# Expert phase of a gated cross-attention chain: 21 blocks of 128 places in place of 14 of 256, weights as the moving operand, the product back in whole fp32

## What is computed

```python
x = hidden_states.reshape(-1, HIDDEN)                 # 896 rows of 256, layer-normed
probs = softmax(30 * tanh(x @ wg.T / 30))             # 8 experts
topk_vals, topk_ids = top_k(probs, 2)
topk_w = topk_vals / sum(topk_vals)
h1 = einsum('th,eih->tei', x, w1)                     # w1, w3: 8 x 1024 x 256
h3 = einsum('th,eih->tei', x, w3)
act = gelu(h1) * h3
out = einsum('tei,ehi->teh', act, w2)                 # w2: 8 x 256 x 1024
# x += tanh(g) * sum of the two chosen experts' rows, weighted
```

## Time and profile before

| | us |
|---|---|
| median of 3 runs | 1394.43 (1383.29 to 1396.78) |
| the profiled execution | 1392.34 |
| span of its instructions | 1390.6 |
| PE busy | 1204.5 (87%) |
| DVE busy | 857.2 (62%) |
| ACT busy | 672.0 (48%) |
| POOL busy | 532.2 (38%) |

### The profile page before, as it was taken

The page is one execution under the profiler, slowest core; times in us unless marked ns, Lnnn a source line. Parts: engine busy times, 40 slices in busy tenths (PEclk is TensorE's granted clock), DMA queues, the critical chain, the costliest instruction groups (busy, mean ns, idle before and its releaser), DMA issues. The chain is left out here.

```text
span 1390.6 us, 25468 instructions
## 1 busy us (share of the span) xinstructions
PE 1204.5 (87%) x9571; PEld 954.4 (69%) x9571; DVE 857.2 (62%) x1973; ACT 672.0 (48%) x1512; POOL 532.2 (38%) x536
## 2 busy tenths in 40 slices
PE   3999999999997697689999469889888859999876
PEld 2677777777775265556777469889887747777544
DVE  6664555555554346667787556666666476777676
ACT  3355444455452221257666234554454136666565
POOL 3355554555553000288887431110100441271132
PEclk9999999999998798889999579999999979999987
DMA  6000000000001151300110355556662260000000
GB/s 181 12 2 12 12 1 12 12 1 1 2 1 29 30 157 41 91 22 23 44 32 2 126 189 167 189 173 200 182 198 83 61 192 24 13 13 2 1 7 21
DMA packets 60090, 88.96 MB, mean 64 GB/s; under 512 B 8673, under 2 KB 49905, under 8 KB 59969
## 3 DMA queue, kind: packets, MB, share of 16 engines
q1 hardware_dynamic: 57856, 81.82, 19.3%
q0 software_dynamic: 2112, 5.51, 1.4%
HBM read 81.81 MB, written 5.51 MB: 63 GB/s over the span
## 5 line engine op out<-in xcount | busy, mean ns | idle before, releaser
L906 POOL TENSOR_SCALAR a_arena<-a_arena 112x487 f32<-112x487 f32 x128 | 192.7, 1516 | 176.9 <-DVE a_arena L1117 176.9
L1198 ACT ACTIVATE a_arena<-banks,a_arena 112x487 f32<-112x487 f32 x128 | 84.2, 663 | 193.0 <-DVE a_arena L1111 193.0
L1111 DVE TENSOR_REDUCE a_arena<-banks 112x2 f32<-112x974 f32 x64 | 75.0, 1172 | 102.6 <-PE banks L997 102.6
L93 PE MATMUL banks<-f_x_high,f_up_high 128*128 128x256 f32 x448 | 128.4, 287 | 3.6 <-DVE f_up_low L2010 2.2
L94 PE MATMUL banks<-f_x_low,f_up_high 128*128 128x256 f32 x448 | 128.0, 286 | 0.0
L95 PE MATMUL banks<-f_x_high,f_up_low 128*128 128x256 f32 x448 | 128.0, 286 | 0.0
L397 POOL TENSOR_TENSOR a_arena<-a_arena 112x375 f32<-112x375 f32 x128 | 114.7, 921 | 24.1 <-ACT a_arena L704 23.9
L513 PE MATMUL banks<-ident,a_arena 112*126 112x112 f32 x768 | 105.5, 274 | 12.0 <-POOL a_arena L397 9.6
L513 PEld LDWEIGHTS banks<-ident,a_arena 112*126 112x126 f32 x768 | 77.2, 143 | 46.0 <-issue 27.6
L2052 POOL DMA_INDIRECT f_arena<-f_rows,f_arena x28 | 32.7, 1167 | 190.8 <-PE banks L2090 172.7
L2216 DVE TENSOR_TENSOR f_arena<-banks,f_arena 128x512 f32<-128x512 f32 x56 | 38.6, 689 | 107.4 <-ACT f_arena L2192 107.4
(11 more groups left out here) (341 smaller groups left out, 3314.0 us busy)
## 6 DMA issues: line engine op xcount, KB each, us to landing
f_arena<-in_L_ffn_w1T SPq DMA_DIRECT2D x14, 1024.0 KB, 5.8
f_arena<-in_L_ffn_w3T SPq DMA_DIRECT2D x14, 1024.0 KB, 4.9
f_arena<-in_L_ffn_w2T SPq DMA_DIRECT2D x14, 1024.0 KB, 5.9
a_arena<-in_ctxT SPq DMA_DIRECT2D x24, 375.0 KB, 5.0
a_arena<-in_ctx SPq DMA_DIRECT2D x16, 375.0 KB
f_y<-f_arena SPq DMA_DIRECT2D x14, 256.0 KB, 5.1
a_arena<-in_L_xattn_Wkv SPq DMA_DIRECT2D x2, 1024.0 KB, 9.9
a_arena<-in_fside_BxSxS SPq DMA_DIRECT2D x8, 164.1 KB, 2.4
```

The costliest lines, as they stand in the source:

```text
L93: pe.matmul(out, sh, mh, start=start, stop=False)
L906: pool.tensor_scalar(z, z, inv[:, n % 4, s:s + 1], None, ALU.mult).then_inc(p_ready, 1)
L1111: dve.tensor_reduce(negmax[:, n % 4, :], banks[0:T, 0:2, 0:KEYS], AX, ALU.max, negate=True).then_inc(max_ready, 1)
L1198: act.activation(prob[n % PR][s][:, 0:KEYS], banks[0:T, s, 0:KEYS], ACT.Exp, bias=negmax[:, n % 4, s:s + 1], accum_out=total[:, n % 4, s:s ...
```

## The change

1. `SIZE` is 128, `BLOCKS` 21. `HALVES` and `GROUPS` are gone.
2. `up(k, j)`, two groups a block: the 128 places are stationary, 512 columns of weights move. A group is 12 matmuls of 512 columns for w1 and w3 together. The result has places on the partitions.
3. So the hidden is transposed: `turn_hidden(n)`, four 128x128 transposes a group into a new PSUM buffer `psH`, moved out by ACT (`move_hidden`). `ps1` and `ps3` go from three banks to two each.
4. The hidden and w2 are no longer split. `down(k)` is eight fp32 matmuls of 256 columns. ACT's and DVE's splitting of the hidden and of w2 goes. w2 is loaded straight into `down_w`, three buffers.
5. w1 and w3 come in halves of 512 KiB into a ring of 12 (`RING`), three blocks deep. A load waits for the split of the half 12 before it; that of w2 for `y_ready` three blocks before.
6. The last two blocks (`LATE = 2`) stay in SBUF, moved out by ACT (`move_late`). Their weights are multiplied into `spread`: `tensor_weights`, 16 small matmuls, and a chain of nine small DVE steps in the routing behind `token`.
7. The indirect gathers of results wait for the store of block 18 (before: block 12).

```diff
@@ class Assignment @@
+        self.psW = ps[:, 384:384 + 3 * late]
+    def tensor_weights(self, pe):
+        pe.wait_ge(self.s_parts_made, 3)
+        for n in range(2 * B):
+            mm = pe.matmul(self.psW, self.hot[:, n, 0:P], self.weights[:, n].rearrange("t j h -> t (j h)"),
+                           start=(n == 0), stop=(n == 2 * B - 1))
+        mm.then_inc(self.s_weights_listed, 1)
...
-        stepped(dve.tensor_tensor(self.last_w, self.inside[:, :, K - 1].rearrange("t (k b) -> t k b", k=2), self.best,
-                                  ALU.mult))
-        dve.tensor_tensor(self.last_weight, self.last_w[:, 0, :], self.last_w[:, 1, :], ALU.add
...
+        for j in range(3):
+            stepped(dve.tensor_copy(self.part[j], whole))
+            settle()
+            if j < 2:
+                stepped(dve.tensor_tensor(self.remain[j], whole, self.part[j], ALU.subtract))
+                whole = self.remain[j]
+                settle()
+            dve.tensor_tensor(self.weights[:, :, j, :], self.inside[:, :, K - self.late:K],
+                              self.part[j].unsqueeze(2).to_broadcast([T, 2 * B, self.late]), ALU.mult
+                              ).then_inc(self.s_parts_made, 1)
+        dve.wait_ge(self.s_weights_listed, 1)
+        dve.tensor_reduce(self.slot_weight, self.psW.rearrange("p (j h) -> p h j", j=3), AX, ALU.add
+                          ).then_inc(self.s_slot_weighted, 1)
@@ def sparse_ffn @@
-    SIZE = 256
-    HALVES = SIZE // P
+    SIZE = P
     BLOCKS = (2 * R + E * SIZE - 1) // SIZE
-    GROUPS = IC // 2
+    LATE = 2
+    HI = I // 2
+    QC = HI // P
+    PART = SLAB // 2
+    RING, DOWN = 12, 3
@@ sync @@
+            def load_up(k, e):
+                for i, z in enumerate(("L2_ffn_w1T", "L2_ffn_w3T") * 2):
+                    n = 4 * k + i
+                    if n >= RING:
+                        wait_low(sp, (n - RING) // 4, (n - RING) % 4)
+                    whole = io[z][bass.ds(e, 1)].rearrange("e (c p) i -> p (e c) i", p=P)
+                    sp.dma_start(raw_part(k, i), whole[:, :, i // 2 * HI:(i // 2 + 1) * HI]
+                                 ).then_inc(raw_loaded[n % RING], 16)
+            def load_down(k, e):
+                if k >= DOWN:
+                    sp.wait_ge(y_ready, k - DOWN + 1)
+                sp.dma_start(down_w[k % DOWN][:], io["L2_ffn_w2T"][bass.ds(e, 1)].rearrange("e (c p) d -> p (e c) d", p=P)
+                             ).then_inc(down_loaded[k % DOWN], 16)
...
+            for k in range(1, BLOCKS):
+                e = sp.value_load(routing.expert[0:1, k:k + 1], min_val=0, max_val=E - 1)
+                load_up(k, e)
+                if k > 1:
+                    load_down(k - 1, last)
+                last = e
+                if 3 < k and k - 4 < BLOCKS - LATE:
+                    store(k - 4)
@@ gpsimd @@
+            pool.wait_ge(routing.s_slot_weighted, 1)
@@ tensor @@
+            def up(k, j):
+                n = 2 * k + j
+                if j == 0:
+                    pe.wait_ge(x_low, k + 1)
+                if n > 1:
+                    pe.wait_ge(gated_done, n - 1)
                 for s, ps in enumerate((ps1, ps3)):
+                    wait_low(pe, k, 2 * j + s)
+                    for c in range(DC):
+                        mm = split_product(pe, ps[n % 2], [z[:, c, :] for z in xs[k % 2]],
+                                           [w[:, s, c, j * HI:(j + 1) * HI] for w in up_w[k % 2]],
+                                           start=(c == 0), stop=(c == DC - 1))
                 mm.then_inc(up_ready, 1)
+            def turn_hidden(n):
+                pe.wait_ge(gated_done, n + 1)
+                if n > 1:
+                    pe.wait_ge(h_moved, n - 1)
+                for c in range(QC):
+                    mm = pe.transpose(psH[n % 2][:, c * P:(c + 1) * P], gated[n % 2][:, c * P:(c + 1) * P], ident[:])
+                mm.then_inc(h_turned, 1)
+            def down(k):
+                pe.wait_ge(h_moved, 2 * k + 2)
+                pe.wait_ge(down_loaded[k % DOWN], 16 * (k // DOWN + 1))
...
+                for c in range(IC):
+                    mm = pe.matmul(psY[:, 0:D], hs[k % 2][:, c, :], down_w[k % DOWN][:, c, :],
+                                   start=(c == 0), stop=(c == IC - 1))
+                mm.then_inc(y_ready, 1)
...
             for k in range(BLOCKS):
+                up(k, 0)
+                if k:
+                    turn_hidden(2 * k - 1)
+                if k + 1 < BLOCKS:
+                    turn(k + 1)
+                up(k, 1)
+                if k:
+                    down(k - 1)
+                turn_hidden(2 * k)
+            turn_hidden(2 * BLOCKS - 1)
+            down(BLOCKS - 1)
@@ scalar @@
             for k in range(BLOCKS):
+                more = k + 1 < BLOCKS
+                gelu(2 * k)
+                if k:
+                    move_hidden(2 * k - 1)
+                if more:
+                    high_rows(k + 1)
+                    split(k + 1, 0)
+                    split(k + 1, 1)
+                gelu(2 * k + 1)
+                if more:
+                    split(k + 1, 2)
+                    split(k + 1, 3)
+                else:
+                    move_late(0)
+                move_hidden(2 * k)
@@ vector @@
             for k in range(BLOCKS):
+                more = k + 1 < BLOCKS
+                gate(2 * k)
+                if k == 1:
+                    tokens()
+                if more:
+                    low_rows(k + 1)
+                    low_weights(dve, k + 1, 0)
+                    low_weights(dve, k + 1, 1)
+                gate(2 * k + 1)
+                if more:
+                    low_weights(dve, k + 1, 2)
+                    if k:
+                        move(k - 1)
+                    low_weights(dve, k + 1, 3)
```

More of the change, by code:

```diff
@@ L1968, in sparse_ffn @@
[L1968 to L1971, removed]
+        hs = [m.sb(f"h{u}", [P, IC, SIZE]) for u in range(2)]
+        raw_place = m.sb("raw", [P, RING * PART])
+        raw = [raw_place[:, j * PART:(j + 1) * PART] for j in range(RING)]
+        gel_place = m.sb("gel", [P, 4 * HI])
@@ L1991, in sparse_ffn @@
         up_ready, gel_done, gated_done = m.sem("up_ready"), m.sem("gel_done"), m.sem("gated_done")
-        h_high, h_low = m.sem("h_high"), m.sem("h_low")
-        y_ready, y_moved, added = m.sem("y_ready"), m.sem("y_moved"), m.sem("added")
+        h_turned, h_moved = m.sem("h_turned"), m.sem("h_moved")
+        down_loaded = [m.sem(f"down_loaded{j}") for j in range(DOWN)]
+        y_ready, y_moved, late_moved, added, finished = (m.sem(n) for n in (
+            "y_ready", "y_moved", "late_moved", "added", "finished"))
@@ L2029, in _ @@
             routing.sync(sp)
-            load(0, 0)
+            load_up(0, 0)
+            load_down(0, 0)
             sp.wait_ge(norm.xn_done, B)
@@ L2050, in gather @@
                     pool.wait_ge(x_turned, k - 1)
[L2051 to L2054, removed]
+                pool.indirect_dma_start(rows[k % 2], None, rows_dram,
+                                        bass.IndirectOffsetOnAxis(routing.token[:, 0, k:k + 1], 0)
+                                        ).then_inc(rows_loaded[k % 2], 16)
             norm.gpsimd_power(pool)
@@ L2058, in _ @@
             pool.memset(zeros, 0.0).then_inc(zeroed, 1)
-            low_weights(pool, 0, 0, 4)
-            low_weights(pool, 0, 1, 4)
+            for i in range(4):
+                low_weights(pool, 0, i, 2)
             pool.wait_ge(x_stored, 16)
@@ L2117, in down @@
                     pe.wait_ge(y_moved, k)
-                if h == 0 and not k:
-                    pe.wait_ge(routing.s_token_made, 1)
+                else:
+                    pe.wait_ge(routing.s_slot_weighted, 1)
                 for c in range(IC):
-                    mm = split_product(pe, psY[:, D * h:D * h + D], [z[:, c, P * h:P * h + P] for z in hs[k % 2]],
-                                       [w[:, c, :] for w in down_w[k % 2]], start=(c == 0), stop=(c == IC - 1))
-                if h:
-                    mm.then_inc(y_ready, 1)
+                    mm = pe.matmul(psY[:, 0:D], hs[k % 2][:, c, :], down_w[k % DOWN][:, c, :],
+                                   start=(c == 0), stop=(c == IC - 1))
@@ new lines, in move_hidden, with move_late @@
+            def move_hidden(n):
+                k, j = n // 2, n % 2
+                act.wait_ge(h_turned, n + 1)
+                if k > 1 and j == 0:
+                    act.wait_ge(y_ready, k - 1)
+                act.copy(hs[k % 2][:, QC * j:QC * (j + 1), :].rearrange("p c s -> p (c s)"), psH[n % 2]
+                         ).then_inc(h_moved, 1)
+            def move_late(h):
+                k = BLOCKS - LATE + h
+                act.wait_ge(y_ready, k + 1)
+                act.wait_ge(y_stored[k % 2], 16 * (k // 2))
+                act.copy(ys[k % 2], psY[:, 0:D]).then_inc(late_moved, 1)
@@ L2205, in _ @@
+            move_hidden(2 * BLOCKS - 1)
```

(1 more changed line is left out.)

263 lines of the change are left out of this document (99 added, 164 removed).

## The result

| | before | after |
|---|---|---|
| median (us) | 1393.9 (4 runs, 1383.3 to 1396.8) | 1315.3 (4 runs, 1309.7 to 1316.8) |
| profiled execution, its span | 1392.3, 1390.6 | 1314.1, 1312.3 |

The ratio is 0.944, 95% interval 0.938 to 0.950. The forecast was 1325, range 1306 to 1352.

What follows compares the result with a forecast made beforehand. PE's instruction stream was taken to bound the loop at 10.6 us a block. The last stored block finishes at 1017.9 instead of 1085.7, 67.8 us less, tail unchanged: 1392.3 - 67.8 = 1324.5, predicted 1325 us, range 1306 to 1352.

Steps and rivals of the forecast that it cites:

- What bounds the loop: Expert loop: PE's instruction stream binds, before with one small stall a block, after at 10.6 us a block.
- Where the gain comes from: Expert loop: fewer places, 2688 instead of 3584, as padding to 128 wastes less; for equal places the new loop is dearer.
- The block: PE in the changed loop: 10.6 us a block of 128, against 19.6 for one of 256.
- transposes 1.1 and switches 0.5: PE's block: ten transposes at 0.11 us each, 1.1; six switches of matmul kind at 0.09 each, 0.5.
- The first block: Start of the loop on PE: 5.5 + 0.3, plus 1.3 for the lower clock level, 7.1 us.
- The start: Before the loop: first gather alone holds block 0, turning and splitting halve; first up at 810.0 instead of 812.99.
- DMA: Loop's loads, gathers and stores: 3.41 MB a block in 9.1 us, below PE's 10.6, halves at 390 GB/s.
- rival D: Loop: DMA at the low rate of 248 GB/s, block 13.8 us, 1386 us; past 1408 at 232 GB/s. Chance 3%.
- The tail: From last stored block finished to DVE's last statistic: stays 29.4 us, set by the gathers.
- B: Loop: a chain between engines stalls PE 1.0 to 1.8 us a block, 1344 to 1359 us. Chance 14%.
- C: Loop: DMA mildly sets the pace, block 11.4 to 12.2 us at 300 to 280 GB/s, 1340 to 1355. Chance 11%.
- E: PE at the lower clock level all through, about 20 us a block, 1500 us. Chance 2%.

Runs made afterwards that it cites:

- two up products: Changed kernel without the third matmul of the split up product: 1299.8 us (0.933); with w2 also loaded only for the first three blocks: 1279.5 us (0.918).
- both experiments on the number of blocks: Changed kernel with 28 blocks of 128 instead of 21: 1384.9 us (0.993); kernel before with BLOCKS = 11, blocks of 256: 1331.6 us (0.955).

## Why the prediction was right, and where it was off

- **What bounds the loop: right.** PE has no idle time; taking work from DMA changed nothing, taking work from PE moved the block to 9.0 and 8.2 us. DVE is busy 6.7 us a block and ACT 6.4 (13.34 and 12.61 of 20 us), where 6.7 and 6.3 were forecast.
- **Where the gain comes from: right.** 20.18 against 19.70 us for 256 places, and both experiments on the number of blocks.
- **The block: 10.6 forecast, 10.09 measured.** Up was 5.5 forecast; the two groups are 5.71 with the longer first distance of each. Down was 3.5 and is 3.46. The term that failed is "transposes 1.1 and switches 0.5": ten transposes and all switches outside up take 0.92, and with the 0.2 inside up 1.1, not 1.6. Six switches at 0.09 were charged on top of transposes already counted at 0.11. One of the six lies between transposes and transposes, and of the others only those from transposes to a split matmul show the extra 0.08 (853.68 to the next start is 0.31, where 0.23 is usual); into transposes (852.88 to 853.11) or into the fp32 matmuls (856.30 to 856.53) it is 0.23 as ever. The whole 0.5 us a block is 9.2 us over 18 blocks, most of what the forecast of the phase was off (67.8 for 79.6).
- **The first block: 7.1 forecast, 8.25 measured** (811.75 to 820.00). I left out `turn_hidden(0)`, 0.4, and charged 1.3 for the lower clock level where its first group took 4.8 instead of 2.8 (granted 0.50 from 811.75 to 815.80). These errors run against those of the other terms.
- **The start: 3.0 forecast, 4.9 measured.** The gathers and the halved turn gave 2.3 and 0.9. The rest, 1.7, is `token` itself. In the trace of before two small steps of DVE (L1875, L1877) took 0.94 and 1.18 us beside POOL's subtraction, in that of after 0.22, since POOL was through with it 2.1 us sooner (15.2 us after the opening statistic instead of 17.3). The wider tables and narrower `hot` rows, forecast to cancel, saved 0.3; an earlier step beside POOL took 0.3 more.
- **DMA: right.** 9.1 forecast; 9.0 at the changed kernel's own 378 GB/s, 9.0 with two up products, 9.0 to 9.2 from w2 loaded twice. The rate that I took for 2 KB runs, 390, holds too: from 840 to 860 of the kernel with hardly any w2 it is 389. The share of the engines reads 1.04 to 1.08 when they are full. The rule of the Trainium skill on small transfers (DMA: Bandwidth & Descriptors, Bandwidth), added up one transfer after another, would have made halves slower than wholes. The trace does not agree: these are queued on SP, where the page's figures are for transfers issued by GpSimd, and they run at 378 against 392 GB/s, with kernel times of 1315.3 and 1316.3 us; neither binds. A slip in rival D: by its sum 232 GB/s gives 1402 us, and 1408 is passed at 227.
- **The tail: size right (27.6 for 29.4), and now its cause is shown** by the kernel with one late block. It was 1.8 us shorter, of which 0.7 is the way from the move to the first gather (3.0 for 3.7).
- B, C, D, E did not happen. C was the nearest: 1.1 us a block were between PE and DMA, and a further MiB a block brought it about, with +40 us. It did not turn into E: PE then waited in 14 of some 17 blocks from 845 to 1050, and the granted clock of the windows from 840 to 1020 stayed between 0.91 and 1.00.

Left open: why the layers ahead of the phase differ by some 7 us from execution to execution. It limits what medians can tell here more than anything in the phase.

## What to carry to other kernels

Count the padding before the instructions: a smaller block pays as long as its per-row cost stays level, and here the wide weights were made the moving side of the matmul for that. (That 128 places as the moving side would have cost more is argued, not shown: no run has it.) Cost every engine for the new block and then the DMA engines by the rate of queued transfers in the kernel's own trace, since the gap to the next bound (10.1 to 9.0 us here) says what a further cut of PE's work is worth. A small store in the queue of the loads can carry their delay to PE, as the results did with w2 loaded twice. And work given to an idle engine is not free: POOL's subtraction and DVE's held each other up, and the copy of w2 held up ACT until its load had landed.

## What was not expected of the hardware

- DVE's and POOL's subtractions with both operands in SBUF take turns, a whole instruction at a time (the rows of the kernel with the product back split up). The wait for the other is inside the recorded duration, 2.32 us where 1.21 is the work, so the busy times overlap in the windows though the work does not. On the mean DVE's take 1.65 us for 1.22 there, and POOL's 1.78 for 1.23.
- TensorE, loaded from SBUF at the full pace, is not slowed by DMA at its limit: an up group of 12 matmuls takes 2.85 us from its first start to the next instruction's at 381 GB/s (900.72 to 903.57 in the changed kernel), and 2.86 at 238 (900.80 to 903.66 with hardly any w2).
